# The start of a one-core transformer kernel: silu and first layer norm on VectorE, first keys spread from ScalarE's queue, large weights loaded behind the first spread

## The reference, cut to what matters

```python
mod = (_silu(L0_c) @ L0_wmod).reshape(L0_c.shape[0], 6, 1, -1)
sa, ca, ga, sb, cb, gb = (mod[:, 0], mod[:, 1], mod[:, 2], mod[:, 3], mod[:, 4], mod[:, 5])
h = _layernorm(x, axis=-1) * (1 + ca) + sa
x = x + ga * _L0_attn_ref(h, W_DKV, W_UK, W_UV, W_UQ, W_O)
h = _layernorm(x, axis=-1) * (1 + cb) + sb
x = x + gb * _L0_ffn_ref(h, wqkv, q_scale, k_scale, wo, ln_g, ln_b, w1, b1, w2, b2)
```

## Time and profile before

| | value |
|---|---|
| median of 3 runs | 2144.49 us (2142.8 to 2147.58) |
| span of the profiled execution | 2140.7 us, 3.8 us under the median |
| PE busy | 1949.1 us, 91% of the span |
| ACT, DVE, POOL busy | 1607.3, 1559.3, 862.1 us |
| mean TensorE clock granted | 0.989 |
| longest part of the chain that ended last | PE, 56% |

### The profile page before, as it was taken

One profiled execution on the slowest core, in us unless ns is written; L12 is line 12 of the kernel. 1 busy time (PEld: TensorE's weight loads), 2 busy tenths in 40 slices (PEclk: granted clock), 3 DMA queues, 4 the chain that ended last, 5 costly groups with the idle time before them and its releaser, 6 DMA issues.

```text
span 2140.7 us, 56185 instructions
## 1 busy us (share of the span) xinstructions
PE 1949.1 (91%) x22308; PEld 1117.7 (52%) x22308; DVE 1559.3 (73%) x2671; ACT 1607.3 (75%) x3975; POOL 862.1 (40%) x826
## 2 busy tenths in 40 slices
PE   6789999999999999999999999999999999999987
PEld 3344545555454655545555554655545455554644
DVE  3476787877778777787877778687777877777753
ACT  1567878787887878777787887878688787877755
POOL 2043616245351624526163361625435162452522
PEclk8999999999999999999999999999999999999999
DMA  4110201213030120202112030120203012030100
GB/s 137 29 32 16 61 7 36 41 24 58 7 68 9 39 43 24 58 7 57 21 32 51 24 58 7 38 39 24 58 7 70 13 36 42 24 53 7 36 6 23
DMA packets 63110, 76.19 MB, mean 36 GB/s; under 512 B 10630, under 2 KB 57856, under 8 KB 60800
## 3 DMA queue, kind: packets, MB, share of 16 engines
q1 hardware_dynamic: 62852, 72.60, 16.1%
HBM read 9.14 MB, written 4.19 MB: 6 GB/s over the span
## 4 chain that ended last, share of the span: by engine, by line
PE 56%; ACT 23%; DVE 12%; issue 5%; SPq 2%; DMA 1%; POOL 1%; DVEq 0%; ACTq 0%; POOLq 0%
PE ps L430 10%; ACT pr L815 6%; PE ps L667 5%; PE ps L564 5%; ACT pr L777 5%; PE ps L594 4%; PE ps L595 4%; PE ps L604 4%; PE ps L658 3%; PE ps L449 3%; ACT pr L788 3%; DVE wm L1000 3%; PE ps L678 2%; PE ps L445 2%; PE ps L687 2%
## 5 line engine op out<-in xcount | busy, mean ns | idle before, releaser
L1091 POOL TENSOR_TENSOR pr<-pr 128x1024 f32<-128x1024 f32 x128 | 302.2, 2361 | 739.7 <-DVE pr L989 739.7
L815 ACT ACTIVATE pr<-ps,wb,inv 128x128 f32<-128x128 f32 x768 | 340.8, 481 | 24.6 <-DVE wb L1006 24.2
L777 ACT ACTIVATE pr<-ps 128x1024 f32<-128x1024 f32 x320 | 314.4, 1028 | 42.5 <-PE ps L449 42.0
L1108 POOL TENSOR_TENSOR pr<-pr,shares 128x512 f32<-128x512 f32 x192 | 199.9, 1048 | 314.0 <-DVE shares L1021 314.0
L947 DVE TENSOR_REDUCE nm<-ps 128x2 f32<-128x256 f32 (+2 forms) x384 | 314.5, 861 | 13.0 <-PE ps L449 11.9
L430 PE MATMUL ps<-cf,pr 128*128 128x128 f32 x1792 | 259.7, 282 | 31.1 <-POOL pr L1108 22.5
L430 PEld LDWEIGHTS ps<-cf,pr 128*128 128x128 f32 x1792 | 200.9, 142 | 124.4 <-issue 55.0
L982 DVE TENSOR_TENSOR pr<-ps,rot 128x1024 f32<-128x1024 f32 x128 | 156.2, 1221 | 120.1 <-ACT pr L788 97.7
L788 ACT ACTIVATE pr<-ps 128x1024 f32<-128x1024 f32 x128 | 131.2, 1025 | 104.6 <-PE ps L595 66.2
L445 PE MATMUL ps<-cb 64*64 64x256 bf16 (+1 forms) x2560 | 175.3, 263 | 30.1 <-ACT pr L777 14.4
L1014 DVE COPY pr<-ps 128x512 f32<-128x512 f32 x256 | 170.1, 679 | 15.2 <-PE ps L430 13.7
(11 more groups left out here) (158 smaller groups left out, 4040.0 us busy)
## 6 DMA issues: line engine op xcount, KB each, us to landing
pr<-V SPq DMA_DIRECT2D x32, 512.0 KB, 4.5
queries<-early SPq DMA_DIRECT2D x224, 64.0 KB
keys<-early SPq DMA_DIRECT2D x224, 64.0 KB
pr<-V SPq DMA_DIRECT2D x32, 384.0 KB, 6.6
xn<-in_L_attn_x SPq DMA_DIRECT2D x16, 256.0 KB, 4.5
out<-hT SPq DMA_DIRECT2D x16, 256.0 KB, 2.2
queries<-mT SPq DMA_DIRECT2D x128, 4.0 KB
Wqkv<-in_L_ffn_wqkv SPq DMA_DIRECT2D x1, 1536.0 KB
```

Of the source, the lines that this page charges most:

```text
L777: act.activation(dst, src, ACT.Exp, scale=SC1).then_inc(ex_r[s], 1)
L815: ins = act.activation(P2[s][2 * (p % 3) + r][:, o:o + P], bank[:, r * T + o:r * T + o + P], ACT.Exp, scale=inv[s][:, t, h:h + 1], bias=wb ...
L1091: pool.tensor_tensor(t1[s][t % 3], t1[s][t % 3], t2[s], ALU.add).then_inc(sum_r[s], 1)
L1108: pool.tensor_tensor(part, part, share, ALU.mult).then_inc(part_r[s], 1)
```

## The change

Four edits, all in the first item's work:

1. Silu and the copy of `Wq` move from DVE's step `plain` of item 0 up into its step `stats` of item 0, so ahead of `stats` of item 1. Behind them DVE also does the four normalising instructions of item 0 that POOL did.
2. The seven DMAs of `Wqkv`, `Wo` and `W2` leave the first loads and their semaphore `ld_late`; SP issues them in its step `proj` 1 of item 0, behind the 14 query spreads, on a semaphore of their own, `ld_rest`. Only PE's step `out` of items 0 and 1 waits for it.
3. The 14 key spreads of item 0 are issued by ACT, at the end of its step `values` of item 0.
4. The filler matmuls of bank turn 2 (two) go, those of turn 7 are 8 in place of 20.

```diff
 FILLS = {
-    2: 2, 7: 20, 17: 7, 69: 10, ...
+    7: 8, 17: 7, 69: 10, ...
-        LATE = 6 + 4 * DEPTH + 2 + 3 * DEPTH + 1
+        LATE = 6 + 4 * DEPTH + 2
+        REST = 1 + 3 * DEPTH
 # PE, step "out"
                         if b < S2:
-                            pe.wait_ge(ld_late, 16 * LATE)
+                            pe.wait_ge(ld_rest, 16 * REST)
 # ACT, step "values"
                         ins.then_inc(v1_r[s], 1)
+                        if b == 0:
+                            for part, done in enumerate((hi_r, mid_r, lo_r)):
+                                act.wait_ge(*done.at(b, 2))
+                                for slot in [k for k in range(SLOTS) if K_PART[k] == part]:
+                                    for r in range(2):
+                                        rows = slice(64 * r + D1 * slot, 64 * r + D1 * (slot + 1))
+                                        act.dma_start(K1[rows, :, :], parts[3 + part][64 * r:64 * r + 64, :]).then_inc(spread_r[s], 16)
 # DVE, step "stats"
                         ins.then_inc(mv_r[n][s], 1)
+                        if b == 0 and n == 0:
+                            dve.wait_ge(filled, 2 + 2 * S2)
+                            dve.wait_ge(ld_kv, 16 * 4)
+                            dve.tensor_copy(Wq[:, :]..., wq_raw...).then_inc(prep_dve, 1)
+                            dve.wait_ge(prep_act, 3)
+                            dve.tensor_scalar(ce, ce, 1.0, None, ALU.add).then_inc(prep_dve, 1)
+                            dve.wait_ge(prep_dve, 2)
+                            dve.reciprocal(cr, ce).then_inc(prep_dve, 1)
+                            dve.wait_ge(prep_dve, 3)
+                            dve.tensor_tensor(csil, cT, cr, ALU.mult).then_inc(prep_dve, 1)
+                            dve.wait_ge(*dev_r[0].at(b, 2))
+                            for t in range(NT):
+                                ins = dve.tensor_scalar(plain[:, t, :], xn[s][:, t, :], mv[0][s][:, t, 0:1], dev[0][s][:, t:t + 1],
+                                                        ALU.subtract, ALU.mult)
+                            ins.then_inc(plain_r[0][s], 1)
-                    elif kind == "plain" and b == 0:
...
 # POOL, step "plain"
-                    if kind == "plain" and a[0] == 0:
+                    if kind == "plain" and a[0] == 0 and b:
...
 # SP, step "proj"
+                        if b == 0 and i == 1:
+                            sp.dma_start(Wqkv[:, :, :], wqkv.rearrange("l c n -> c l n")).then_inc(ld_rest, 16)
+                            for l in range(DEPTH):
+                                sp.dma_start(Wo[:, l, :, :], wo[l].rearrange("(a p) n -> p a n", p=P)).then_inc(ld_rest, 16)
+                                sp.dma_start(W2[:, l, 0:2, :], w2[l, 0:2 * P, :].rearrange("(c p) n -> p c n", p=P)).then_inc(ld_rest, 16)
+                                sp.dma_start(W2[0:HID - 2 * P, l, 2, :], w2[l, 2 * P:HID, :]).then_inc(ld_rest, 16)
+                            return
```

More of the change, by code:

```diff
@@ L335, in build @@
         ps = ctx.enter_context(nc.psum_tensor("ps", [P, BANKS, T], F32))
-        ld_const, ld_cond, ld_kv, ld_mask, ld_late = (sem(f"init_{n}") for n in ("const", "cond", "kv", "mask", "late"))
+        ld_const, ld_cond, ld_kv, ld_mask, ld_late, ld_rest = (sem(f"init_{n}") for n in ("const", "cond", "kv", "mask", "late", "rest"))
         zeroed, filled = sem("init_zeroed"), sem("init_filled")
@@ L868, in step @@
                         ins.then_inc(mv_r[n][s], 1)
+                        if b == 0 and n == 0:
+                            dve.wait_ge(filled, 2 + 2 * S2)
+                            dve.wait_ge(ld_kv, 16 * 4)
+                            dve.tensor_copy(Wq[:, :].rearrange("p (r d q) -> p r d q", r=2, d=D1),
+                                            wq_raw.rearrange("p (q r d) -> p r d q", r=2, d=D1)).then_inc(prep_dve, 1)
+                            dve.wait_ge(prep_act, 3)
[9 more added lines that the diff above has]
+                            ins.then_inc(plain_r[0][s], 1)
                     elif kind == "plain" and a[0] == 1:
@@ L1058, in step @@
                     s = b % S2
-                    if kind == "plain" and a[0] == 0:
+                    if kind == "plain" and a[0] == 0 and b:
                         pool.wait_ge(*dev_r[0].at(b, 2))
-                        if b:
-                            pool.wait_ge(*v1_r.at(b - 1, 1))
-                            pool.wait_ge(*hi_r.at(b - 1, 2))
+                        pool.wait_ge(*v1_r.at(b - 1, 1))
+                        pool.wait_ge(*hi_r.at(b - 1, 2))
                         for t in range(NT):
@@ L1180, in _ @@
                 sp.dma_start(Wo1[:, :], wo1).then_inc(ld_late, 16)
[L1181 to L1185, removed]
                 sp.dma_start(B2[:, :], b2.rearrange("l p -> p l"), allow_slow_non_contiguous=True).then_inc(ld_late, 16)
```

## The result

The changed kernel is slower: 2155.18 us median (2153.24 to 2157.81, 5 runs) against 2145.05 us for the kernel before on the same chip, a ratio of 1.0047 with a 95% interval of 1.0036 to 1.0058. The forecast was 2135.8 us, with a range of 2132.5 to 2140.5.

A forecast was written before the change was run, and what follows sets the result against it. PE, busy for 91% of the span, bounds the kernel; the change moves when its pipeline starts. First max from 43.58 to 34.9 us saves 8.7: span 2140.7 to 2132.0, plus 3.8 around it, 2135.8 us; range 2132.5 to 2140.5.

The forecast's parts named there:

- Silu, norm, turn 2: First item's start: silu ready at 9.25 us, norm costs and saves nothing, transposes near 12.9 us, 2.5 us earlier.
- The issues on ACT: Item 0's 14 key spreads on ACT: 0.65 us each, from 20.45 to 29.6 us.
- Rival (d): ACT's key issues cost over 1.2 us each; at 1.77 us, first max near 50 us, time 2151 us; chance 0.04.
- Item 1's projections: PE's work behind ACT's issues: 2.85 to 4.8 us, so first max not before 33.5 to 35.4 us; 34.9 taken.
- What the DMA engines carry: Two spread streams at share 0.40 each make 0.80 and fit; keys land at 32.3 us, or 38.8 behind all weights.
- (c): Spreads use half the DMA engines, two streams 1.25 times one; keys land at 35 to 41 us, 2139.5 us; chance 0.12.
- (b): The weights hold up the key spreads: landing at 37 to 39 us, end time 2138.9 us; chance 0.13.
- The sum: First max from 43.58 to 34.9 us saves 8.7 us, nothing behind it, 1.5 us either way for the clock.
- The 12 fillers of turn 7: On PE before item 1's transposes: 8 fillers take 2.4 to 3.5 us, covered by ACT's issues; 20 would cost one to two.
- Around the span: Time outside the profiled span: 3.8 us, added to span 2132.0 for 2135.8 us.

The follow-up runs named there:

- c_weights_last: The changed kernel, but SP issues the large weights only after all spreads of item 0 have landed: 2148.58 us, ratio 1.0014 to the kernel before.
- a_keys_on_sp: The changed kernel with item 0's key spreads back on SP behind the query spreads, large weights behind both: 2148.28 us, ratio 1.0010.
- f_small_first_keys_sp: As e_small_first, but the key spreads are issued by SP behind the queries: 2146.44 us, ratio 1.0005.
- e_small_first: The changed kernel with the large weights again among the first loads, last, behind `B2`; keys from ACT: 2143.13 us, ratio 0.9988.
- j: As c_weights_last, with 20 fillers at turn 7 and 20 ahead of the first max: 2146.86 us, ratio 1.0009.
- i: As e_small_first, with 20 fillers at turn 7 and 6 ahead of the first max: 2142.80 us, ratio 0.9988.
- k: As g, with 20 fillers at turn 7 and 8 ahead of the first max: 2142.28 us, ratio 0.9986.
- b: The changed kernel with the large weights again among the first loads, ahead of `B2`; keys from ACT: 2146.74 us, ratio 1.0005.
- g: As c_weights_last, but `Wqkv` is issued ahead of the query spreads: 2144.02 us, ratio 0.9993.
- h: As e_small_first, but SP and ACT wait for the large weights' landing before the first spread: 2154.06 us, ratio 1.0044.
- m: As h, but both streams write their slots in order 0 to 6: 2158.77 us in one execution, beside 2146.39 of the kernel before.

## Why the prediction was wrong, step by step

**Silu, norm, turn 2.** Right in kind, and nearly in size. Silu at 9.45 us (said 9.25), transposes at 13.23 (12.9), query spread from 18.03 (17.6). 0.3 us of it are the loads, which landed later in this execution: PE's first transposes began at 7.66 us, in place of 7.35.

**The issues on ACT.** Right in kind: 0.65 us each was said, 10.81 us for 14 is 0.77: the first one took 1.46, while ACT's copies ran, and the other 13 some 0.72 each. They ended at 31.6 and not 29.6. Rival (d), issues of over 1.2 us, didn't come. That it had the first max near 50 us and the time at 2151 is no merit of it: ACT's issues were over 18 us before the first max.

**Item 1's projections.** They ended at 36.15 + 1.92 = 38.07 us, all at the low level; I had said 33.5 to 35.4. Two microseconds are ACT's issues, and the rest the loads and PE's level. So even without the rest the first max would have been at 38.1 us, and the gain 5.5 us and not 8.7.

**What the DMA engines carry.** This is the step that failed. "Two streams would be 0.80, and that still fits" took a share in one state of the engines as the price of the bytes in any. The price per byte was that of spreads behind a bulk load, and the change took this load away from in front of them. Without it, the spreads cost 0.121 us per KB in place of 0.065, and the landing that I had put at 32.3 us came, in c_weights_last, at 43.5 without any weights among them. The sum of shares was wrong for fast spreads too: two streams behind a load had a share of 0.56 and 1.3 to 1.7 times the rate of one. The weights themselves were bounded rightly: I allowed them up to 6.5 us, and 5.5 to 6.2 is what they cost. But I added this to 32.3 us, and in the forecast it was to be hidden under item 1's projections. Both signs that I had named for the rivals came: a share stuck near 0.5, (c), and then one near 1 with a late landing, (b). But neither rival had a rate lower than that of one stream, so no case of mine reached past 2141.5 by way of a transfer (2141.9, if its 41 us is taken from 43.58). The only slower case I had was the issue cost.

The rows were there to be read. In the kernel before, the spreads of the second item start on idle engines: their share is 0.01 from 60 to 84 us. The timeline of SP's queue and a stretch around these spreads show:

```profile
90.20 9.56 SPq L1136 DMA_DIRECT2D queries<-early  x14
99.87 9.08 SPq L1136 DMA_DIRECT2D keys<-early  x14
```
```profile
90.00:110.00 20.00, 16.17 (x83) 7.49 (x83) 7.82 (x22) 4.40 (x8) 0.34 (x1) 0.93 0.46 85
```

The issues took as long as those of the first item, so SP's queue shows nothing. But 0.46 at 85 GB/s is 0.087 us per KB, and from 100 to 108 us, at a share of 0.57 and 90 to 92 GB/s, it is 0.100. I priced from the first item alone.

These later spreads also bound the theory. After an idle start they have 90 to 92 GB/s and not the 75 to 78 of a_keys_on_sp, so an idle start alone doesn't set the rate. And traffic directly ahead isn't always enough:

```profile
502.66 0.60 SPq L1148 DMA_DIRECT2D pr<-V  x1
503.36 11.26 SPq L1136 DMA_DIRECT2D keys<-early  x14
```

Here the key spreads stand right behind two copies of V inside SBUF. From 504 to 506 us the engines have a share of 0.90 with 194 GB/s, but from 510 to 514 us the spreads move 75 to 76 GB/s at 0.57 to 0.58. What is shown is the effect of the loads from HBM in this beginning; no run tests what it is in such a load that helps.

The Trainium skill (DMA: Bandwidth & Descriptors, section "Issuing engines are not separate DMA queues") says that a second issuer saves only the time of issuing. The traces agree: where one stream left room (100 GB/s at 0.40 in f_small_first_keys_sp), issues from ACT beside those of SP raised the rate to 139 to 172 GB/s; where the engines were the limit (0.58), one stream had 75 to 78 GB/s and two had 77. The rule on how many engines a copy uses (same page of the Trainium skill, section "Why a DMA increments its semaphore by 16 and not by 1") would give these copies 8 of 16 engines. No run here shows single engines. But the share of pure spread traffic that is backed up stays at 0.55 to 0.60 in every kernel here, at 64 GB/s as at 172, near half of what full engines read (0.98 to 1.09), which fits that rule.

**The sum.** The prediction charged nothing behind the first max and 1.5 us for the clock. The first max came 6.2 us late and the median 10.1. Up to the second norm of item 0 the shift did carry over one to one, as said: 107.63 us in place of 101.22 is 6.4 us, and in c 101.35 is 0.1. The rest is lost behind that. At SP's load of `x` at 387.90 us the shift is 9.7 us, and 3.7 in c. But e_small_first loses as much there, its lead shrinks from 5.7 to 2.3 us, so this part isn't the price of the late keys; and the profiled execution of the kernel before was itself a fast one (see below), so some of it is that execution. From 40 to 150 us the granted clock was 0.82, against 0.91 before. PE had nothing to do from 38.1 to 49.8 us, and that idle time lies in this stretch; over the 106.4 us that follow the first max the clock was 0.85 against 0.90. The 12 fillers of turn 7 that I called covered may be part of what kept it up, but no run puts back these 12 alone. c and j put about 1 us of 3 on the clock. In the changed kernel the rest of the 4 us isn't taken apart.

**Around the span.** I took 3.8 us for it. Executions of the experiments have 1.8 us (2148.56 us with a span of 2146.8). So the profiled execution of before took about 2142.5 us (an estimate), 2 to 3 us under its median, and spans compared with it make a changed kernel look that much worse: 12.1 us by the spans, 10.1 by the medians.

**What the change was worth.** Its silu, norm and filler edits, with `B2` ahead of the weights, move the first max by 1.2 us and the time not measurably (f). Key spreads from ACT are worth 3.3 us on top of that (2146.44 to 2143.13), if the weights stay in front. Moving the weights behind the spreads turns the 0.9988 of e_small_first into the 1.0047 of the changed kernel, 0.59% or 12.7 us. Best measured are e, i and k, 0.12 to 0.14% under the kernel before, and not apart from each other.

## What to carry to other kernels

A DMA share read from one stretch prices only transfers that start in the same state: before moving a load, find the same transfers in the trace both behind other traffic and on idle engines, and compare share per GB/s. Don't move bulk loads behind latency-bound copies on the ground alone that they then come later, but time both orders; here, ahead of the copies, the loads were drained in time and the copies ran at twice the rate. And when a beginning is shortened by letting TensorE idle, read the granted clock of the next hundred microseconds as part of the price.

## What the runs showed of the hardware

- Copies of 64 partitions x 1 KB into 8 partitions (64 KB each), in the first item: one stream 99 to 100 GB/s behind a load from HBM (before, f); two streams from SP and ACT 131 to 172 GB/s behind such a load (b, e, g); one or two streams 68 to 78 GB/s when started on idle or nearly idle DMA engines (the changed kernel, a, c, h), and 64 in m. In the second item of the kernel before, after an idle start, 90 to 92 GB/s.
- A bulk load that joins such slow copies is slow itself: 133 to 139 GB/s for both at a full share (the changed kernel, a), in place of 381 with the load alone, and 5.5 to 6.2 us more for the copies (the changed kernel against c).
- Issuing one of them costs 0.61 us on SP alone, and 0.70 us (median of 14) on ACT while SP issues too.
- The 88 executions of the kernel before spread over 2140.4 to 2149.5 us, and the mean granted clock (0.991 to 0.984) goes with that.
